# Gated delta-rule heads on one Trainium2 core: decay rows by a broadcast DMA, tail decay on the keys, half-size fillers and a new order of a head step

## What is computed

```python
mixed = silu(causal_conv(x @ w_qkv, conv_w)); q, k, v = split(mixed)
beta, g = sigmoid(x @ w_b), -exp(A_log) * softplus(x @ w_a + dt_bias)
def step(state, q_t, k_t, v_t, g_t, b_t):      # per token and value head
    state = state * exp(g_t)
    delta = (v_t - k_t @ state) * b_t
    state = state + outer(k_t, delta)
    return state, q_t @ state
o = rmsnorm(outs * silu(x @ w_z)) * gamma;  y = o @ w_out
```

## Time and profile before

| | us |
|---|---|
| runs (3) | 1463.66, 1465.13, 1470.07 |
| median | 1465.13 |
| profiled execution: span from its first to its last instruction | 1464.3 |
| of it, before the first scan step | 96.8 |
| 14 scan steps with all kinds of work | 846.7 |
| the last two scan steps | about 96.5 |
| MLP, attention, experts | 424.3 |
| busy in the span: PE, DVE, ACT, POOL | 1315.5, 963.0, 792.5, 752.4 |

### The profile page before, as it was taken

How to read it: one execution, slowest core, us unless ns; L and a number is a source line. 1 busy time by engine, 2 the same in 40 slices (tenths; PEclk the granted TensorE clock), 3 DMA queues, 4 the chain that set the end, 5 groups by cost and what they waited for, 6 DMA issues and landing times. The chain is left out here.

```text
span 1464.3 us, 24950 instructions
## 1 busy us (share of the span) xinstructions
PE 1315.5 (90%) x8680; PEld 880.2 (60%) x8680; DVE 963.0 (66%) x1922; ACT 792.5 (54%) x1947; POOL 752.4 (51%) x1245
## 2 busy tenths in 40 slices
PE   5768999999999999999999999988898899599994
PEld 3356666666666666666666666665545466455673
DVE  5857777778787787877878778665603466531454
ACT  4546766676666766767667576664422455310121
POOL 1775775856858568586685766841000000125363
PEclk9879999999999999999999999999998999789997
DMA  3434356364463544545445445355003930033487
GB/s 88 126 63 113 71 146 148 84 161 100 131 149 92 164 89 130 145 101 156 112 115 137 112 145 117 94 154 169 22 0 118 335 101 1 2 116 107 100 187 189
DMA packets 233180, 171.71 MB, mean 117 GB/s; under 512 B 163746, under 2 KB 202998, under 8 KB 230240
## 3 DMA queue, kind: packets, MB, share of 16 engines
q1 hardware_dynamic: 226912, 161.59, 40.7%
q0 software_dynamic: 6144, 8.53, 3.3%
HBM read 104.64 MB, written 65.83 MB: 116 GB/s over the span
## 5 line engine op out<-in xcount | busy, mean ns | idle before, releaser
L1267 DVE SCALAR_TENSOR_TENSOR heads_y<-psum_banks,gdn_conv_w,heads_y 128x1021 f32<-128x1021 f32 (+2 forms) x192 | 244.7, 1275 | 9.3 <-ACT heads_y L1072 4.8
L776 PE MATMUL psum_banks<-main_hT,gdn_w_in 128*128 128x512 f32 x512 | 242.5, 608 | 6.2 <-DMA gdn_w_in<-in_w_in 4.0
L1562 POOL TENSOR_TENSOR heads_XT<-heads_XT,heads_tmp 128x126 f32<-128x126 f32 (+22 forms) x496 | 207.8, 419 | 38.9
L1559 POOL TENSOR_TENSOR heads_tmp<-heads_XT,heads_A 128x126 f32<-128x126 f32 (+22 forms) x496 | 180.0, 363 | 39.9
L776 PEld LDWEIGHTS psum_banks<-main_hT,gdn_w_in 128*128 128x128 f32 x512 | 97.1, 195 | 95.5 <-issue 91.4
L1530 POOL TENSOR_TENSOR heads_og<-heads_og,heads_fac 128x512 f32<-128x512 f32 x60 | 60.5, 1041 | 137.5 <-DVE heads_fac L1333 137.5
L890 PE MATMUL psum_banks<-heads_w_z,main_hT 128*128 128x256 f32 x512 | 121.8, 381 | 0.0
L1095 ACT ACTIVATE heads_O<-psum_banks,heads_coef 128x128 f32<-128x128 f32 x224 | 70.0, 364 | 95.6 <-PE psum_banks L807 95.2
L1072 ACT ACTIVATE heads_y<-psum_banks,gdn_conv_w 128x1024 f32<-128x1024 f32 x64 | 71.5, 1117 | 91.7 <-PE psum_banks L776 91.7
L1288 DVE SCALAR_TENSOR_TENSOR heads_S<-heads_S,heads_coef,psum_banks 128x128 f32<-128x128 f32 x192 | 57.3, 340 | 86.9 <-PE psum_banks L830 86.4
L1278 DVE SCALAR_TENSOR_TENSOR heads_X<-psum_banks,heads_coef,heads_v_s 128x128 f32<-128x128 f32 x224 | 67.9, 345 | 65.2 <-PE psum_banks L805 65.2
...
...
## 6 DMA issues: line engine op xcount, KB each, us to landing
...
heads_v_s<-values_by_tokens SPq DMA_DIRECT2D x16, 1024.0 KB, 5.5
outputs_by_features<-heads_ogT SPq DMA_DIRECT2D x120, 128.0 KB, 2.6
...
heads_A<-kk_blocks SPq DMA_DIRECT2D x64, 128.0 KB, 4.8
keys_by_tokens<-heads_k_tok SPq DMA_DIRECT2D x64, 128.0 KB, 3.3
```

The lines of the kernel that those rows point to most:

```text
L776: ins = pe.matmul(out[:, half * 512:(half + 1) * 512], w_in[:, kd_, j * P:(j + 1) * P], hT[:, kd_, half * 512:(half + 1) * 512], start=kd_ ...
L1267: dve.scalar_tensor_tensor(y[j][:, shift:T], src[:, 0:T - shift], conv_w[:, head, j, t:t + 1], y[j][:, shift:T], ALU.mult, ALU.add).then_i ...
L1559: pool.tensor_tensor(tmp[:, 0:n, 0:m], bc_last(XT[:, 0:n, j], m), bc_mid(A0[:, j, j + 1:BLK], n), ALU.mult).then_inc(solve_step.sem, 1)
L1562: pool.tensor_tensor(XT[:, 0:n, j + 1:BLK], XT[:, 0:n, j + 1:BLK], tmp[:, 0:n, 0:m], ALU.add).then_inc(solve_step.sem, 1)
```

## The change

Four things change in the head steps, and nothing outside them.

1. *Decay rows.* The two small tiles and the 16 matmuls go. SP loads the head's 16 x 128 cumulative gates straight into `Dm`, the same 8 KB for every partition (1 MB written). DVE adds the mask, in SBUF. ACT takes the exponential with the negative cumulative gate of the token as a bias per partition, so 128 columns at a time, 16 instructions. As `Dm` is the DMA's target, the DMA of head h waits until `inverse1` of step h-1 is done, and `decay0` of step h waits for it.
2. *Tail decay.* `Dt` goes. ACT scales the keys of the chunk by the decay ahead of time into `k_tail` (two buffers, two instructions per chunk), and `su` is two matmuls of 128 columns with these as weights and `Dl` as the moving side.
3. *Halves.* A name such as `p1.0` or `z1.1` is half of a filler product (0.85 us of it), so that a row of the table can hold half of one.
4. *Order.* All five plans are new.

```diff
 PE_PLAN = banked(rows("""
...
-6: decay0/3 decay1/2 decay2/0 decay3/1
...
+1: p0/-1 p1.0/-1
+2: p1.1/-1 z1.0/2
...
 DVE_PLAN = rows("""
-0: kt variance
...
+0: decay0
+1: kt
+3: variance decay1 tap00 tap01
...
-SP_PLAN = """kt_out inverse_out kt_in inverse_in values_out products_out values_in products_in gates
-outputs_out0 outputs_in0 outputs_out1 outputs_in1 w_z w_in w_o""".split()
-POOL_PLAN = """pow q_root norm0 norm1 norm2 norm3 scale solve""".split()
+SP_PLAN = """gates inverse_out values_out inverse_in products_out values_in products_in outputs_out0 w_z kt_out outputs_in0 outputs_out1 outputs_in1 w_in kt_in w_o""".split()
+POOL_PLAN = """pow norm0 norm1 q_root scale norm2 norm3 solve""".split()
...
             def gate_rows(h):
-                for sign, rows in enumerate([row_to, row_from]):
-                    src = cum_rows[sign, IT * h:IT * (h + 1)].rearrange("(g s) t -> g s t", g=4)
-                    sp.dma_start(rows[h % 2][sign:P:32], src).then_inc(s_rows[h % 2], 16)
+                src = cum_rows[IT * h:IT * (h + 1)].rearrange("(o s) t -> o (s t)", o=1)
+                sp.dma_start(flat(Dm[:]), src.to_broadcast([P, IT * P])).then_inc(rows_in.sem, 16)
...
                 elif name == "gates":
-                    b = bank_of(h, "decay3")
-                    sp.wait_ge(full[b].sem, full[b].done(h, "decay3"))
-                    gate_rows(h + 2)
+                    sp.wait_ge(uf_ready.sem, uf_ready.end(h - 1))
+                    gate_rows(h)
...
                     if c < C - 1:
-                        if c == 0:
-                            pe.wait_ge(kt_loaded.sem, kt_loaded.end(h - 1) * 16)
-                        pe.wait_ge(dt_ready.sem, dt_ready.done(h, f"dt{c}"))
-                        pe.matmul(flat(bank_a[:, 0:2]), k_tok[old][:, c], flat(Dt[:]), start=True, stop=True).then_inc(a_full.sem, 1)
+                        pe.wait_ge(tail_ready.sem, tail_ready.done(h, f"kt{c}"))
+                        for e in range(HD):
+                            ins = pe.matmul(bank_a[:, e], k_tail[c % 2][:, e], Dl[:, e], start=True, stop=True)
+                        ins.then_inc(a_full.sem, 1)
...
-                elif name == "decay0":
-                    for s in range(4):
-                        for g in range(4):
-                            r, out = slice(32 * g, 32 * g + 2), bank[bank_of(h, f"decay{g}")]
-                            ins = pe.matmul(out[:, s], row_from[par][r, s], row_to[par][r, s], start=True, stop=True)
...
+            def tail_keys(h, c):
+                if c > 1:
+                    act.wait_ge(a_full.sem, a_full.done(h, f"su{c - 2}"))
+                elif h > 1:
+                    act.wait_ge(a_full.sem, a_full.base(h))
+                for e in range(HD):
+                    i = c * HD + e
+                    ins = act.activation(k_tail[c % 2][:, e], k_tok[(h - 1) % 2][:, c], ACT.Copy, scale=coef[:, TAIL, h - 1, i:i + 1])
+                ins.then_inc(tail_ready.sem, 1)
...
+                    if c == 0:
+                        act.wait_ge(kt_loaded.sem, kt_loaded.end(h - 1) * 16)
+                        tail_keys(h, 0)
                     act.wait_ge(a_full.sem, a_full.done(h, f"tx{c}"))
                     act.activation(flat(Dl[:]), flat(bank_a[:, 0:2]), ACT.Copy).then_inc(dl_ready.sem, 1)
-                    if c < C - 1:
-                        for e in range(HD):
-                            i = c * HD + e
-                            ins = act.activation(Dt[:, e], bank_a[:, e], ACT.Copy, scale=coef[:, TAIL, h - 1, i:i + 1])
-                        ins.then_inc(dt_ready.sem, 1)
+                    if c + 1 < C - 1:
+                        tail_keys(h, c + 1)
...
                 if name.startswith("exp"):
-                    b = bank_of(h, f"decay{u}")
-                    act.wait_ge(free[b].sem, free[b].done(h, f"decay{u}"))
-                    part = flat(Dm[:, 4 * u:4 * u + 4])
-                    act.activation(part, part, ACT.Exp).then_inc(dm_ready.sem, 1)
+                    act.wait_ge(dm_masked.sem, dm_masked.done(h, str(u)))
+                    for it in range(4 * u, 4 * u + 4):
+                        ins = act.activation(Dm[:, it], Dm[:, it], ACT.Exp, bias=coef[:, NCUM, h, it:it + 1])
+                    ins.then_inc(dm_ready.sem, 1)
...
+                if name.startswith("decay"):
+                    dve.wait_ge(rows_in.sem, rows_in.end(h) * 16)
+                    part = Dm[:, 4 * u:4 * u + 4]
+                    dve.tensor_tensor(part, part, bc_mid(limit[:], 4), ALU.add).then_inc(dm_masked.sem, 1)
+                    return
...
-                elif name.startswith("decay"):
-                    dve.wait_ge(full[b].sem, full[b].done(h, name))
-                    dve.tensor_tensor(Dm[:, 4 * u:4 * u + 4], bank[b][:], bc_mid(limit[:], 4), ALU.min).then_inc(free[b].sem, 1)
```

More of the change, by code:

```diff
@@ L205 @@
 0: z0/0
-1: p0/-1 p1/-1
-3: z1/1
-4: z2/2 norm_q/3
-5: p2/-1
-6: decay0/3 decay1/2 decay2/0 decay3/1
-7: p3/-1 kk0/3
-8: attn0/1 kk1/3
-9: attn1/2
-10: y6a/3 y6b/0
-12: p4/-1
-13: p5/-1 u6a/3 u6b/0
-14: z3/1
-16: y7_0/0 p6/-1 p7/-1
-18: y7_1/3 u7_0/0
-19: out0/2
-20: u7_1/3
-21: out1/1
-22: out2/2 out3/1
+1: p0/-1 p1.0/-1
+2: p1.1/-1 z1.0/2
+3: z1.1/2 z2.0/1
+4: norm_q/3 z2.1/1
+5: p2.0/-1
+6: p2.1/-1
+7: p3/-1
+8: kk0/2 kk1/3
+9: attn0/1
+10: attn1/2 y6a/3 y6b/0
+11: p4.0/-1
+12: p4.1/-1
+13: p5/-1
+14: u6a/3 u6b/0 z3/1
+15: y7_0/3
+16: p6/-1
+17: p7.0/-1
+18: p7.1/-1
+19: y7_1/1 u7_0/3
+20: out0/2
+21: out1.0/0
+22: out1.1/0 out2/3 u7_1/2 out3/1
 """))
@@ L291 @@
 DVE_PLAN = rows("""
-0: kt variance
-2: tap00
-3: tap01 tap02
-4: vt0 norm_q
-5: vt1 decay0 decay1 decay2
-6: decay3
-8: tap10 tap11 tap12 factors turn
-11: ot0 attn0
-13: scales tap20
-14: tap21 tap22 attn1
-15: ot1
-19: tap30
-20: inverse0 out0 tap31 out1
-22: out2 tap32 inverse1 out3
+0: decay0
+1: kt
+3: variance decay1 tap00 tap01
+4: tap02
+5: vt0 vt1
+6: norm_q
+7: decay2 factors
+9: tap10 tap11 turn
+10: tap12
+11: attn0
+12: decay3 ot0
+13: attn1 scales
+15: tap20 tap21 tap22
+18: ot1
+20: tap30
+21: inverse0 out0 tap31 out1
+22: inverse1 out2 tap32 out3
 """)
@@ L335, in belongs @@
         return h == HK + 1
-    if name in ("w_in", "gates"):
+    if name == "w_in":
         return h + 2 < HK
+    if name == "gates":
+        return h in INVERT and h > 0
     if name == "w_z":
@@ L353, in plan, with unit @@
     return {0: PE_FIRST, 1: PE_SECOND, HK + 1: PE_LAST}.get(h, PE_PLAN)
+def unit(name):
+    return name.partition(".")[0]
 def bank_of(h, name):
-    return next(b for row in plan(h) for n, b in row if n == name)
+    return next(b for row in plan(h) for n, b in row if unit(n) == name)
 def bank_plan(h, bank):
-    return [name for row in plan(h) for name, b in row if b == bank and belongs(h, name)]
+    return list(dict.fromkeys(unit(name) for row in plan(h) for name, b in row if b == bank and belongs(h, name)))
 def pe_row(h, k):
@@ L451, in heads @@
     z = a.sb("z", [P, C, HD * P])
-    row_from = [a.sb(f"row_from{i}", [P, 4, P]) for i in range(2)]
-    row_to = [a.sb(f"row_to{i}", [P, 4, P]) for i in range(2)]
     limit = a.sb("limit", [P, P])
@@ L478, in heads @@
     Dl = a.sb("Dl", [P, HD, P])
-    Dt = a.sb("Dt", [P, HD, P])
+    k_tail = [a.sb(f"k_tail{i}", [P, HD, P]) for i in range(2)]
     og = [a.sb(f"og{i}", [P, IT, P]) for i in range(2)]
@@ L852, in product @@
                     pe.wait_ge(act_ready.sem, act_ready.done(h, "sq"))
-                elif name == "decay0":
-                    pe.wait_ge(s_rows[par], 32 * (h // 2 + 1))
-                    for g in range(1, 4):
-                        more = free[bank_of(h, f"decay{g}")]
-                        wait(pe, more, more.ahead(h, f"decay{g}"))
                 elif name.startswith("flip"):
```

122 lines of the change are left out of this document (65 added, 57 removed).

## The result

The changed kernel takes 1517.5 us (median of 4 runs, 1509.8 to 1524.9) against 1465.0 before: a ratio of 1.036, interval 1.031 to 1.040. The forecast was 1448 in a range of 1412 to 1484, and the time is outside it. The profiled execution took 1524.9 us, its span is 1522.8.

A forecast was written before the change was run, and what follows sets the result against it. It took PE's work to bound a step. Thirds summing to 30.5 + 28.6 = 59.1 us save 1.24 us a step, 17.4 over 14; 1464.3 - 17.4 + 1 = 1447.9, stated as 1448, range 1412 to 1484.

The forecast's parts named there:

- The load of the rows: SP's 1 MB DMA into Dm at the step's start: taken to land 5.5 us after issue, at 6.0.
- rival A: At the border on SP's queue: rows land late, 7.5 us, step 61.2 us, 1480 in all; chance 22%.
- First third: From tx to p2: DVE's row is longest behind the rows' load, p2 at 15.55 instead of 14.29, 1.26 us lost.
- Second third: From p2 to p4: PE's work 14.54 us, DVE's and the inverse load's row about equal; p4 at 30.5 instead of 31.17.
- the wait of 1.24 us: PE's longest wait, for ACT's copy Dl ahead of `o` in the second third; booked as removed by half products.
- Last third: From p4 to the next tx: 28.6 us instead of 29.17, as order and halves can remove a 0.70 us wait.
- Rival B: No change: DVE's masks wait for POOL, exponentials precede a Dl copy; 0.7 and 0.6 us per step, 1465; chance 20%.
- The exponentials: On ACT, 16 narrow for 4: at most 3.4 us more per step, hidden; up to 0.9 us if ahead of Dl.
- The tail decay: k_tail on ACT and su as two matmuls on PE: no gain booked, cost 0, at worst 0.7 us per step.
- Step 15: The step after the 14 full ones: with less PE filler to cover the load, it loses some 2 us.
- The gain of 17 us: Over the 14 full steps: 1.24 us less per step, 59.1 instead of 60.34, 17.4 us in all.
- rival C: Larger gain: rows land in 4.2 us or less, both long PE waits go, 3.04 us per step, 1422; chance 16%.

The follow-up runs named there:

- x1: Changed kernel with the inverse's load ahead of the values' store again in SP's list; 1466.3 us, ratio 1.003 to the kernel before.
- b2: Changed kernel's decay rows and tail decay in the five plans of before, without half products; 1502.8 us, ratio 1.027 to the kernel before.
- b3: Kernel before with the tail decay alone (k_tail for Dt, su as two matmuls); 1463.8 us, ratio 1.001.
- b4: b2 with ACT's narrow exponentials spread behind the Dl copies of chunks 3 and 4; 1490.1 us, ratio 1.019 to the kernel before.
- x4: x1 with DVE's fourth mask behind the third and its first mask behind the copy of S and gate; 1461.2 us, ratio 0.999 to the kernel before.
- x11: x4 with GpSimd's second pair of output norms back ahead of the scaling of the values; 1440.3 us, ratio 0.985 to the kernel before.
- x13: x1 with GpSimd's second pair of output norms back ahead of the scaling of the values; 1452.2 us, ratio 0.991 to the kernel before.
- k1: b4 with one unused 512-column matmul on PE ahead of the y6 products; 1487.2 us, ratio 1.017 to the kernel before.

## Why the prediction was wrong

*The load of the rows* was right: 5.1 us (4.5 to 7.1) against 5.5 forecast. Slower was rival A's direction, but its mechanism, a late load, did not come about.

*First third:* 15.16 us against 15.55. DVE's walk was right within 0.2 us for each instruction, and the wait ahead of the second `ks` was where it was said to be. One premise was wrong without harm: `inverse1` moved ahead of one add and one tap, not two adds, as `out3` stood behind it before too. It waits 2.30 us for ACT, and that it still ended at 0.15 us, near the 0.2 forecast, is luck.

*Second third* is the step that failed. I set p4 by DVE's row (30.5) and PE's work (14.54 us after p2) as two rows that end at about the same time, and booked the wait of 1.24 us as gone. The walk had the turn done at 27.9; measured 28.5. But the y6 products, which read the turn, stand on PE ahead of p4, and PE reaches them at 26.0. I did not put the turn against the place of its reader. So a wait of 2.05 us a step (28.7 / 14) took the place of the one removed, and p4 stands at 31.22. x1, where the turn does not wait, gives PE's own row: p4 follows p2 by 609.03 - 595.39 = 13.64 us there, 0.9 less than my 14.54, while the load's row took 31.22 - 15.16 = 16.06, against 14.95 forecast. I had the two 0.4 us apart; they were 2.4 apart. x1 shows this as the cause: one list entry, 51 us.

*Last third:* 28.6 forecast, 31.46 measured, the larger miss in this step, and most of it a consequence of the late turn: in the step of x1 shown above, with neither block nor fall, it is 29.35. Two terms were missing. The fourth mask falls into GpSimd's scaling of the values and takes up to 4.06 us. Rival B had this mechanism, but bounded its price by GpSimd's add of 0.42, and so at 0.7 us a step; I did not look which of GpSimd's instructions stands there. By the rule quoted from the Trainium skill, "SBUF — State Buffer", section Who interferes with whom, the mask waits until the other is done. The trace agrees: GpSimd's instruction begins 0.44 us earlier and ends at 640.58, and the mask 0.54 us after it. Where the mask begins first, as in the twelfth step, it keeps its 0.68 us and GpSimd's instruction takes 4.03 in place of 3.64:

```profile
829.30 0.68 DVE L1394 TENSOR_TENSOR heads_Dm<-heads_Dm,heads_limit 128x512 f32<-128x512 f32 x1
829.45 4.03 POOL L1567 TENSOR_TENSOR heads_v_s<-heads_v_s,heads_k_root 128x2048 f32<-128x2048 f32 x1 [8.97 <-DMA heads_v_s<-values_by_tokens]
```

And the clock, which the forecast held at 0.99 without a price for a fall, was at 0.95: 34 us more lost than before.

*The exponentials* were booked as free, with 0.9 us where they stand ahead of Dl. They take 78.1 / 16 = 4.9 us a step against 2.4. In the order of before two groups stand there and cost 1.27 us (b2); the new order avoids that (PE's waits for Dl in its 14 steps are 2.0 us in all), which is a gain of the order that I did not see. With the tail decay worth nothing (b3), the rows cost 39 us in the order of before; their exponentials' place ahead of Dl explains 13 of it (b4), and the rest is open.

*The tail decay* was right at nothing (b3). *Step 15* was booked with 2 us and cost 12.

*The gain of 17 us* did not come even without the wait. In x1 eight of the 14 steps do take 57.9 to 59.1 us; the others have a fall of the clock or are the first two (63.5 and 61.4), and step 15 takes 6.7 more than before. What held x1 to x4 was GpSimd's order, by x11 and x13, most likely as a loop over its elimination and SP's list, which the forecast did not walk at all. With the norms moved (x11) a step from the third on takes 57.6 us in the mean, less than the 59.1 forecast and near the 57.3 of rival C, though not by its quick landing.

What stays open: why the clock falls in only half of the steps of b2, though the wait of 2.51 us stands in every one, and in every step of b4 behind 1.02 us; and what sets the 61.4 us of a step in b4 and k1.
